# Attention scores of four heads in two pairs, with the first pair's maxima ahead of the Mamba scan

## The chip, the cores and the metric

One NeuronCore of one Trainium2 chip runs the whole kernel as one program. The metric is device time in microseconds (us), here the median of several executions; lower is better.

Five engines work side by side, each through its own list of instructions in the order written: PE (matrix multiplies and transposes, in the trace split into the multiply PE and its weight load PEld), DVE (vector), ACT (scalar), POOL (GpSimd) and SP (it only issues DMAs here). They meet through semaphores: an instruction raises a counter when it has finished (`then_inc`), and another engine's list stops at `wait_ge` until the counter is high enough. What stands behind a wait in a list waits too.

## The reference

One decoder layer, float32, batch 4, sequence 256, hidden 256. Three blocks, each followed by a residual add and a layer norm:

```python
x = layernorm(x + attention(x))               # 16 heads of 16, causal softmax, Wo at the end
x = layernorm(x + mamba(ctx, gate=silu(x)))   # conv + selective scan, 256 channels, 16 states, length 256
x = layernorm(x + moe(x))                     # softmax router, top 2 of 8 experts, 512 inner
```

In the attention, `scores = Q K^T / 4` under a causal mask, `attn = softmax(scores)`, `out = attn V`. In the scan, for each of 256 channels and 16 states, `state_t = exp(delta_t * A) * state_(t-1) + delta_t * u_t * B_t`, and `y_t = sum over states of state_t * C_t`.

## The kernel before

The attention and the scan don't depend on each other, so the kernel interleaves them. The main part is a loop over 4 batches `b` and, inside, 8 steps `m`; `g = 8*b + m` numbers the steps, and each step scans two of the 16 states. In steps m = 0 to 3 of a batch the four groups of heads, `G = 4*b + m`, are also scored: a group has four heads `r`, each with its own PSUM bank of `psS`. There is no scheduler. The order on each engine is written out by hand in one loop per engine, and what follows is what the change touches.

PE, step m: `scores(G)` writes the causal mask into the four banks with four matmuls (L1357, one per head, each waiting for that head's exponentials of the group before, since these read the bank), then adds QK^T for queries 0 to 127 (L1361) and for queries 128 to 255 (L1365), four heads each, every head on its own 32 rows of the array, and raises `score_ps` once. Then `broadcast_b(g+1, n)` (L1337) spreads B of the next step's two states over the partitions into `psD[n]`; it waits for the scan (g, n), which reads the same bank. Then `turn_back(G-2)` (L1397) and `transpose_probs(G-1, j)` for j = 0, 1, 2 (L1379), each of which waits until ACT has copied the previous one out of `psT`, and `weigh_values(G-1)` (L1390).

DVE, step m: `multiply_b(g)` (L972, two halves) multiplies `psD` by delta*u; `scan(g)` (L981, two instructions) runs the recurrence from `psD` into `states`; `maxima(G)` takes the negated row maxima of all four heads in two reduces (L987 for 128 keys, L988 for 256 keys) and raises `max_rdy` once. Behind them come, by step, `add_gated` (L1036), `finish_delta`, `normalise` (L994, L995) and `gating` (L1026). Only in the very first step do the maxima stand ahead of the scan.

ACT, step m: `decay(g+2)` (L689) makes the scan's decay factors; then, in turn, `take_probT(G-1, 0)` (L727, the copy out of `psT`), `exponentials(G, 0)` (L718 and L719), `take_probT(G-1, 1)`, `exponentials(G, 1)`, `take_probT(G-1, 2)`, `exponentials(G, 2)` and `(G, 3)`, and `take_o(G-1)` (L731). Each `exponentials(G, r)` waits for `max_rdy`, that is for the maxima of all four heads.

POOL, step m: `multiply_c(g)` (L504 and on) takes the states that the scan left, and now and then the small layer norm operations (`inverse_deviation`, L491 to L494), which ACT's `normalise_rows` (L740) waits for.

After the loop come the router, the sorting of tokens to experts and 23 tiles of expert work, which the change doesn't touch.

Of the kernel before, what the change touches and what calls it, by code (L numbers as in the profile page):

```python
# [10 lines left out]
ALU = mybir.AluOpType  # L11
ACT = mybir.ActivationFunctionType
AX_X = mybir.AxisListType.X

P = 128
# [35 lines left out]
def decoder_layer(  # L51
# [28 lines left out]
    B, S, HID = x.shape  # L80
# [13 lines left out]
    SCORE = P + S  # L94
# [6 lines left out]
    GROUPS = 4  # L101
    GH = HEADS // GROUPS
# [10 lines left out]
    with ExitStack() as stack:  # L113
# [14 lines left out]
        ident_b = sb("ident_b", [P, P], BF16)  # L128
        mask_qk = sb("mask_qk", [P, P], BF16)
# [42 lines left out]
        q_m = sb("q_m", [P, 2, FC, S])  # L172
        k_sb = sb("k_sb", [P, FC, S])
        v_sb = sb("v_sb", [P, QC, HEADS, BC])
        negmax = sb("negmax", [P, 2, QC, GH])
# [417 lines left out]
        def _(act):  # L593
# [117 lines left out]

            def exponentials(G, r):
                H = GH * G + r
                act.wait_ge(max_rdy, G + 1)
                if G >= 2:

                    act.wait_ge(probT_ps, 3 * (G - 1))
                act.activation(probs_q[:, H % PR, 0:P], psS[:, r, 0:P], ACT.Exp, bias=negmax[:, G % 2, 0, r:r + 1])  # L718
                act.activation(probs_q[:, H % PR, P:], psS[:, r, P:SCORE], ACT.Exp,  # L719
                               bias=negmax[:, G % 2, 1, r:r + 1]).then_inc(prob_rdy, 1)  # L720
# [38 lines left out]
            for b in range(B):  # L759
                f = b - 1  # L760
                for m in range(NP):
                    g = NP * b + m
# [104 lines left out]
        def _(dve):  # L867
# [106 lines left out]
            def scan(g):  # L974
                if g >= ST:

                    dve.wait_ge(y_sum, g - ST + 1)
                for n in range(2):
                    dve.wait_ge(b_used, 2 * g + n + 1)
                    dve.wait_ge(dA_rdy, 4 * g + 2 * n + 2)  # L980
                    dve.tensor_tensor_scan(  # L981
                        states[:, g % ST, n].rearrange("p h s -> p (h s)"), dA[:, g % DA, n].rearrange("p h s -> p (h s)"),
                        psD[:, n, :], 0.0, ALU.mult, ALU.add).then_inc(scanned, 1)

            def maxima(G):
                dve.wait_ge(score_ps, G + 1)
                dve.tensor_reduce(negmax[:, G % 2, 0], psS[:, :, 0:P], AX_X, ALU.max, negate=True)  # L987
                dve.tensor_reduce(negmax[:, G % 2, 1], psS[:, :, P:SCORE], AX_X, ALU.max, negate=True).then_inc(max_rdy, 1)  # L988

            def normalise(G):  # L990
                t, a = divmod(G % GROUPS, 2)
# [53 lines left out]
            for b in range(B):  # L1045
                f = b - 1
                for m in range(NP):
                    g = NP * b + m
                    multiply_b(g)
                    if g == 0:  # L1050
                        maxima(0)
                    scan(g)
                    if m == 3 and f >= 0:
                        add_gated(f)
                    if 0 < m < GROUPS or g > 0 and m == 0:
                        maxima(GROUPS * b + m)
                    if 0 < g < B:
                        finish_delta(g)
                    if 2 <= m <= 5:
                        normalise(GROUPS * b + m - 2)  # L1060
                    if m == 1 and f >= 0:
                        gating(f)
                    elif m == 6:
                        if f >= 0:
                            take_logits(f)
                    elif m == 7:
                        residual(b)
# [172 lines left out]
        def _(pe):  # L1240
# [99 lines left out]
            def scores(G):  # L1340
                b, g = divmod(G, GROUPS)
                t, a = divmod(g, 2)
                if g == 0:
                    pe.wait_ge(q_rdy, 2 * (b + 1))
                    pe.wait_ge(k_rdy, b + 1)
                    pe.wait_ge(v_rdy, b + 1)
                    if b > 0:
                        pe.wait_ge(res_rdy, b)
                if G == 0:
                    pe.wait_ge(mask_rdy, 1)  # L1350
                    pe.wait_ge(abs_rdy, TH)
                    pe.wait_ge(relu_rdy, TH * HALVES)
                for r in range(GH):
                    if g > 0:

                        pe.wait_ge(prob_rdy, GH * (G - 1) + r + 1)
                    pe.matmul(psS[:, r, 0:2 * S].rearrange("p (j n) -> p j n", n=S)[:, :, 0:P], ident_b[:],  # L1357
                              mask_qk[:].rearrange("p (o n) -> p o n", o=1).broadcast_to([P, 2, P]), start=True, stop=True)
                for r in range(GH):
                    rows = slice(32 * r, 32 * r + 32)  # L1360
                    pe.matmul(psS[:, r, 0:P], q_m[rows, a, t, 0:P], k_sb[rows, t, 0:P], start=False, stop=True,  # L1361
                              skip_group_check=True)
                for r in range(GH):
                    rows = slice(32 * r, 32 * r + 32)
                    ins = pe.matmul(psS[:, r, P:SCORE], q_m[rows, a, t, P:S], k_sb[rows, t, :], start=False, stop=True,  # L1365
                                    skip_group_check=True)
                ins.then_inc(score_ps, 1)

            def take_turn(use):

# [321 lines left out]
```

## Time and profile before

| what | value |
|---|---|
| median of 3 runs (lowest, highest) | 428.7 us (428.37, 428.83) |
| the profiled execution, its own time | 431.48 us |
| its span, first to last instruction | 429.7 us |
| busy: PE, DVE, POOL, ACT | 340.4, 252.1, 248.5, 209.9 us |
| mean granted TensorE clock | 0.878 of full speed |
| loop over batches and steps, by DVE's first multiply to its last scan | about 34 to 237 us |
| expert work | about 270 to 406 us |

Busy time is time in instructions, without waits. In the loop (half of the span) no engine is always busy, so what counts there is which engine waits for which, and when. In the timeline rows of the section below the columns are: start and length in us, engine, line, operation, what it writes and reads, how many instructions the row merges, and in brackets how long the engine had stood idle before it and who released it. In rows by stretch they are: the stretch, its length, busy us (and count) of PE, PEld, DVE, ACT and POOL, the granted clock as a share of full speed, DMA share and GB/s. In rows of waits: engine, tile and line that waited, for whom, total us, times, longest. SPq means DMAs that SP issues.

### The profile page before, as it was taken

To read this page: it belongs to the slowest core of one execution; us is meant where nothing else is said; L and a number is where in the kernel's file an instruction comes from. 1 tells how busy PE (TensorE), PEld (TensorE's weight loads), DVE (VectorE), ACT (ScalarE), POOL (GpSimd) and SP (SyncE) were. 2 spreads that over 40 slices of the span, in tenths; PEclk is the share of its full clock that TensorE was granted. 3 is DMA by queue.
4 is the path that set the end of the run, shared out by engine and by line. 5 is a ranking of instruction groups with operands and counts; after the bars stand their busy time and mean duration, and the time that the engine had idled before them with its cause. 6 is when DMAs were issued, how large, how long until landed. Compare 5 with 4: busy or idle time off the path is not lost.

```text
span 429.7 us, 5678 instructions
## 1 busy us (share of the span) xinstructions
PE 340.4 (79%) x1780; PEld 205.5 (48%) x1780; DVE 252.1 (59%) x439; ACT 209.9 (49%) x488; POOL 248.5 (58%) x232
## 2 busy tenths in 40 slices
PE   8794868856778677875869586899999999999651
PEld 4352435623446244653435242466666666666441
DVE  2989797974958879688977676112122222222134
ACT  4678786737877678767964100322222222212103
POOL 2075999999978996789888302233233333331214
PEclk9986596965989769896986888999999999999967
DMA  7050110162114510242106950111111111111162
GB/s 209 8 101 3 38 35 31 47 219 50 50 50 82 188 50 26 65 148 84 51 24 218 374 193 0 49 41 46 37 51 49 50 49 37 50 37 38 37 195 99
DMA packets 29455, 34.46 MB, mean 80 GB/s; under 512 B 4074, under 2 KB 23826, under 8 KB 29426
## 3 DMA queue, kind: packets, MB, share of 16 engines
q1 hardware_dynamic: 24770, 26.36, 20.3%
q0 software_dynamic: 2208, 6.03, 4.6%
q10 hardware_dynamic: 2448, 1.71, 1.4%
q8 instruction: 15, 0.25, 0.2%
q14 instruction: 14, 0.11, 0.1%
HBM read 28.92 MB, written 5.18 MB: 79 GB/s over the span
## 4 chain that ended last, share of the span: by engine, by line
PE 36%; DVE 6%; DMA 2%; ACT 2%; POOL 2%; issue 2%; DVEq 0%; POOLq 0%; ACTq 0%
PE psS L1600 18%; PE psD L1619 5%; PE psO L1619 4%; PE psD L1610 2%; PE psS L1450 2%; PE psT L1595 1%; DMA c_rows<-z_out 1%; DVE experts L981 1%; POOL rstd L493 1%; DVE u_sb L1131 1%; PE psT L1379 1%; DMA delta<-x_rows,row_in 1%; DMA z_out<-delta,row_out 1%; PE psT L1444 0%; POOL rstd L492 0%
## 5 line engine op out<-in xcount | busy, mean ns | idle before, releaser
L1600 PE MATMUL psS<-experts,delta 128*128 x184 | 86.5, 593 | 0.5 <-ACT delta L818 0.5
L504 POOL TENSOR_TENSOR experts<-experts,c_rows 128x1024 f32<-128x1024 f32 x31 | 73.0, 2355 | 17.8 <-DVE experts L981 17.4
L981 DVE TENSOR_TENSOR_SCAN experts<-experts,psD 128x512 f32<-128x512 f32 x64 | 74.4, 1204 | 0.0
L572 POOL DMA_INDIRECT z_out<-delta,row_out x23 | 22.8, 991 | 88.4 <-ACT delta L832 88.4
L1379 PE MATMUL psT<-ident,probs_at 128*128 128x128 f32 x192 | 39.2, 340 | 23.4 <-ACT probT L727 23.4
L1205 DVE COPY u_sb<-psD 128x512 f32<-128x512 f32 x23 | 15.9, 692 | 68.7 <-PE psD L1610 68.7
L689 ACT ACTIVATE experts<-delta,A_sb 128x255 f32<-128x255 f32 x128 | 54.7, 517 | 0.5 <-DVE du L929 0.5
L972 DVE TENSOR_TENSOR psD<-du,psD 128x512 f32<-128x512 f32 x64 | 41.6, 688 | 13.2 <-PE psD L1337 12.9
L1600 PEld LDWEIGHTS psS<-experts,delta 128*128 128x128 f32 x184 | 33.1, 190 | 24.3 <-issue 23.3
L1379 PEld LDWEIGHTS psT<-ident,probs_at 128*128 128x128 f32 x192 | 27.4, 172 | 35.1 <-ACT probT L727 33.4
L507 POOL TENSOR_TENSOR experts<-experts 128x512 f32<-128x512 f32 x31 | 40.7, 1312 | 2.4
L515 POOL TENSOR_TENSOR y_sb<-y_sb,experts 128x512 f32<-128x512 f32 x31 | 39.8, 1282 | 2.4
L727 ACT COPY probT<-psT 128x512 f32<-128x512 f32 x48 | 28.2, 587 | 22.3 <-PE psT L1379 21.2
L1213 DVE TENSOR_TENSOR du<-du,psS 128x512 f32<-128x512 f32 x23 | 15.8, 688 | 37.2 <-PE psS L1600 37.2
L1337 PE MATMUL psD<-bc_parts,rows_b 96*128 96x512 bf16 x64 | 25.5, 454 | 9.2 <-DVE experts L981 9.0
L719 ACT ACTIVATE probs_at<-psS,negmax 128x256 f32<-128x256 f32 x64 | 31.0, 484 | 0.0
L718 ACT ACTIVATE probs_at<-psS,negmax 128x128 f32<-128x128 f32 x64 | 24.1, 377 | 12.3 <-DVE negmax L988 11.8
L566 POOL DMA_INDIRECT delta<-x_rows,row_in x23 | 22.6, 982 | 10.1 <-issue 6.8
L825 ACT ACTIVATE du<-psS 128x512 f32<-128x512 f32 x23 | 13.7, 598 | 29.5 <-PE psS L1600 29.5
L1357 PE MATMUL psS<-mask_qk,ident_b 128*128 128x256 bf16 x64 | 15.1, 332 | 12.4 <-ACT probs_at L719 9.0
L1619 PE MATMUL psD<-experts,u_sb 128*128 x96 | 22.8, 380 | 0.9 <-DVE u_sb L1205 0.9
L832 ACT COPY delta<-psD 128x256 f32<-128x256 f32 x12 | 4.5, 372 | 36.7 <-PE psD L1619 36.7
(236 smaller groups left out, 591.6 us busy)
## 6 DMA issues: line engine op xcount, KB each, us to landing
c_rows<-c_dram SPq DMA_DIRECT2D x32, 256.0 KB, 3.4
experts<-in_L_ffn_w_gate_dram SPq DMA_DIRECT2D x8, 512.0 KB, 5.9
experts<-in_L_ffn_w_up_dram SPq DMA_DIRECT2D x8, 512.0 KB, 6.9
experts<-in_L_ffn_w_down_dram SPq DMA_DIRECT2D x8, 512.0 KB, 8.1
x_in<-in_x_dram SPq DMA_DIRECT2D x4, 256.0 KB, 5.3
x_rows<-x_sb SPq DMA_DIRECT2D x4, 256.0 KB, 2.5
probs_at<-z_out SPq DMA_DIRECT2D x4, 256.0 KB, 5.1
c_rows<-z_out ACTq DMA_DIRECT2D x4, 256.0 KB, 6.3
```

The costliest lines, as they stand in the source:

```text
L504: pool.tensor_tensor(states[:, g % ST], states[:, g % ST], c_rows[:, g % CR].rearrange("p n (o s) -> p n o s", o=1).broadcast_to([P, 2, HA ...
L507: pool.tensor_tensor(states[:, g % ST, 0], states[:, g % ST, 0], states[:, g % ST, 1], ALU.add).then_inc(pair_rdy, 1)
L515: pool.tensor_tensor(y_sb[:, b % 2], y_sb[:, b % 2], states[:, g % ST, 0], ALU.add).then_inc(y_sum, 1)
L689: act.activation(dA[:, g % DA, n, half, 1:], delta[:, b, half, 1:], ACT.Exp, scale=A_sb[:, half, 2 * m + n:2 * m + n + 1]).then_inc(dA_rdy, 1)
L719: act.activation(probs_q[:, H % PR, P:], psS[:, r, P:SCORE], ACT.Exp, bias=negmax[:, G % 2, 1, r:r + 1]).then_inc(prob_rdy, 1)
L727: act.copy(probT[:, j], psT[:].rearrange("p (h n) -> p h n", h=GH)).then_inc(psT_taken, 1)
L972: dve.tensor_tensor(halves(psD[:, n, :]), du[:, b], halves(psD[:, n, :]), ALU.mult).then_inc(b_used, 1)
L981: dve.tensor_tensor_scan(states[:, g % ST, n].rearrange("p h s -> p (h s)"), dA[:, g % DA, n].rearrange("p h s -> p (h s)"), psD[:, n, :], ...
L1337: pe.matmul(halves(psD[:, n, :]), pick(2 * m + n), wide(bc_parts[:, b * S:(b + 1) * S]).broadcast_to([3 * BC, HALVES, S]), start=True, sto ...
L1379: ins = pe.transpose(psT[:, r * P:(r + 1) * P], probs_q[:, (GH * G + r) % PR, j * P:(j + 1) * P], ident[:])
L1600: ins = pe.matmul(psS[:, bank, :], xgT[:, s % 2, k, :], gate_up_of(bass.ds(e, 1), i)[:, k, :], start=(k == 0), stop=(k == FC - 1))
L1619: ins = pe.matmul(y_bank(s), hgT[:, s % 2, c, :], down_of(bass.ds(e, 1))[:, c, :], start=(c == 0), stop=(c == IC - 1))
```

## The change

Each group of four heads is now handled in two pairs, heads 0 and 1, then heads 2 and 3. PE does mask, QK^T of the first query half and of the second for a pair and raises `score_ps`, then does the same for the other pair; the wait on the previous group's exponentials is one per pair. DVE takes a pair's maxima in two reduces of half the size, and raises `max_rdy` once per pair. The first pair's maxima stand between `multiply_b(g)` and `scan(g)`, the second pair's directly behind `scan(g)` (before, all four stood behind the scan, and in m = 3 behind `add_gated` too). ACT's exponentials of heads 0 and 1 wait for the first pair's maxima, those of heads 2 and 3 for the second's.

```diff
             def exponentials(G, r):
                 H = GH * G + r
-                act.wait_ge(max_rdy, G + 1)
+                act.wait_ge(max_rdy, 2 * G + r // 2 + 1)
...
-            def maxima(G):
-                dve.wait_ge(score_ps, G + 1)
-                dve.tensor_reduce(negmax[:, G % 2, 0], psS[:, :, 0:P], AX_X, ALU.max, negate=True)
-                dve.tensor_reduce(negmax[:, G % 2, 1], psS[:, :, P:SCORE], AX_X, ALU.max, negate=True).then_inc(max_rdy, 1)
+            def maxima(G, pair):
+                heads = slice(2 * pair, 2 * pair + 2)
+                dve.wait_ge(score_ps, 2 * G + pair + 1)
+                dve.tensor_reduce(negmax[:, G % 2, 0, heads], psS[:, heads, 0:P], AX_X, ALU.max, negate=True)
+                dve.tensor_reduce(negmax[:, G % 2, 1, heads], psS[:, heads, P:SCORE], AX_X, ALU.max,
+                                  negate=True).then_inc(max_rdy, 1)
...
                     multiply_b(g)
-                    if g == 0:
-                        maxima(0)
+                    if m < GROUPS:
+                        maxima(GROUPS * b + m, 0)
                     scan(g)
+                    if m < GROUPS:
+                        maxima(GROUPS * b + m, 1)
                     if m == 3 and f >= 0:
                         add_gated(f)
-                    if 0 < m < GROUPS or g > 0 and m == 0:
-                        maxima(GROUPS * b + m)
...
-                for r in range(GH):
+                for pair in ((0, 1), (2, 3)):
                     if g > 0:
 
-                        pe.wait_ge(prob_rdy, GH * (G - 1) + r + 1)
-                    pe.matmul(psS[:, r, 0:2 * S].rearrange("p (j n) -> p j n", n=S)[:, :, 0:P], ident_b[:],
-                              mask_qk[:].rearrange("p (o n) -> p o n", o=1).broadcast_to([P, 2, P]), start=True, stop=True)
-                for r in range(GH):
-                    rows = slice(32 * r, 32 * r + 32)
-                    pe.matmul(psS[:, r, 0:P], q_m[rows, a, t, 0:P], k_sb[rows, t, 0:P], start=False, stop=True,
-                              skip_group_check=True)
-                for r in range(GH):
-                    rows = slice(32 * r, 32 * r + 32)
-                    ins = pe.matmul(psS[:, r, P:SCORE], q_m[rows, a, t, P:S], k_sb[rows, t, :], start=False, stop=True,
-                                    skip_group_check=True)
-                ins.then_inc(score_ps, 1)
+                        pe.wait_ge(prob_rdy, GH * (G - 1) + pair[1] + 1)
+                    for r in pair:
+                        pe.matmul(psS[:, r, 0:2 * S].rearrange("p (j n) -> p j n", n=S)[:, :, 0:P], ident_b[:],
+                                  mask_qk[:].rearrange("p (o n) -> p o n", o=1).broadcast_to([P, 2, P]), start=True, stop=True)
+                    for r in pair:
+                        rows = slice(32 * r, 32 * r + 32)
+                        pe.matmul(psS[:, r, 0:P], q_m[rows, a, t, 0:P], k_sb[rows, t, 0:P], start=False, stop=True,
+                                  skip_group_check=True)
+                    for r in pair:
+                        rows = slice(32 * r, 32 * r + 32)
+                        ins = pe.matmul(psS[:, r, P:SCORE], q_m[rows, a, t, P:S], k_sb[rows, t, :], start=False, stop=True,
+                                        skip_group_check=True)
+                    ins.then_inc(score_ps, 1)
```

What this makes of PE's order in a step with scores is shown for m = 2. Before, from the scores of the group to the values (`rows_b` and `bc_parts` are the operands of the broadcast of B):

```order
L1357 MATMUL psS<-mask_qk,ident_b 128x2x128 x4
L1361 MATMUL psS<-k_sb,q_m 128x128 x4
L1365 MATMUL psS<-k_sb,q_m 128x256 x4
L1337 MATMUL psD<-bc_parts,rows_b 128x512 x2
L1397 MATMUL psO<-ident,oT_sb 128x128 x2
L1379 MATMUL psT<-ident,probs_at 128x128 x12
```

The same place now (lines 1360, 1364, 1368 are those of mask and QK^T in the changed kernel, L1339 is the broadcast, L1400 and L1382 are `turn_back` and the transposes):

```order
L1360 MATMUL psS<-mask_qk,ident_b 128x2x128 x2
L1364 MATMUL psS<-k_sb,q_m 128x128 x2
L1368 MATMUL psS<-k_sb,q_m 128x256 x2
L1360 MATMUL psS<-mask_qk,ident_b 128x2x128 x2
L1364 MATMUL psS<-k_sb,q_m 128x128 x2
L1368 MATMUL psS<-k_sb,q_m 128x256 x2
L1339 MATMUL psD<-bc_parts,rows_b 128x512 x2
L1400 MATMUL psO<-ident,oT_sb 128x128 x2
L1382 MATMUL psT<-ident,probs_at 128x128 x12
```

The three rows of scores became six; the broadcasts, `turn_back` and the transposes stand behind them as before.

DVE in the same step m = 2 of a later batch, before (L981, the scan, is listed as SCALAR_TENSOR_TENSOR):

```order
L972 TENSOR_TENSOR psD<-du,psD 128x512 x2
L981 SCALAR_TENSOR_TENSOR experts<-experts,psD 128x512 x2
L987 TENSOR_REDUCE negmax<-psS 128x4
L988 TENSOR_REDUCE negmax<-psS 128x4
L994 RECIPROCAL recip<-psO 128x8
L995 TENSOR_TENSOR o_sb<-psO,recip 128x2x4x16
```

And now:

```order
L972 TENSOR_TENSOR psD<-du,psD 128x512 x2
L988 TENSOR_REDUCE negmax<-psS 128x2
L989 TENSOR_REDUCE negmax<-psS 128x2
L981 SCALAR_TENSOR_TENSOR experts<-experts,psD 128x512 x2
L988 TENSOR_REDUCE negmax<-psS 128x2
L989 TENSOR_REDUCE negmax<-psS 128x2
L996 RECIPROCAL recip<-psO 128x8
L997 TENSOR_TENSOR o_sb<-psO,recip 128x2x4x16
```

Two reduces, with a wait for the first pair's scores in front of them, moved from behind the scan to ahead of it.

## Rows read from the trace of the kernel before

**Rows 1.** Who waited for whom, whole span, three of the rows

```profile
PEld psD L1337 <- DVE experts L981: 14.3, 14, 5.4
DVE negmax L987 <- PE psS L1365: 14.0, 7, 4.6
...
ACT probs_at L718 <- DVE negmax L988: 11.8, 7, 3.2
```

**Rows 2.** Busy time by stretch: the whole of batch 2

```profile
138.70:190.00 51.30, 38.52 (x272) 24.02 (x272) 41.62 (x62) 38.26 (x96) 43.24 (x34) 0.83 0.26 81
```

**Rows 3.** Timeline of batch 2, step m = 2 and the start of m = 3

```profile
153.34 2.32 DVE L981 TENSOR_TENSOR_SCAN experts<-experts,psD 128x512 f32<-128x512 f32 x2
...
155.39 1.03 PE L1357 MATMUL psS<-mask_qk,ident_b 128*128 128x256 bf16 x4
...
158.02 0.69 DVE L987 TENSOR_REDUCE negmax<-psS 128x4 f32<-128x512 f32 x1 [2.36 <-PE psS L1365]
...
158.63 1.22 DVE L988 TENSOR_REDUCE negmax<-psS 128x4 f32<-128x1024 f32 x1
159.18 0.59 ACT L727 COPY probT<-psT 128x512 f32<-128x512 f32 x1 [1.42 <-PE psT L1379]
...
163.33 0.70 PE L1357 MATMUL psS<-mask_qk,ident_b 128*128 128x256 bf16 x4
163.55 0.40 ACT L731 COPY oT_sb<-psO 128x256 f32<-128x256 f32 x1
...
164.82 0.61 PE L1337 MATMUL psD<-bc_parts,rows_b 96*128 96x512 bf16 x2
...
166.12 0.59 ACT L727 COPY probT<-psT 128x512 f32<-128x512 f32 x1 [0.58 <-PE psT L1379]
...
170.81 0.40 ACT L731 COPY oT_sb<-psO 128x256 f32<-128x256 f32 x1
```

**Rows 4.** Timeline of batch 2, step m = 0

```profile
139.44 0.60 PE L1357 MATMUL psS<-mask_qk,ident_b 128*128 128x256 bf16 x4 [0.94 <-ACT v_sb L709]
139.89 2.33 DVE L981 TENSOR_TENSOR_SCAN experts<-experts,psD 128x512 f32<-128x512 f32 x2
139.97 0.50 PE L1361 MATMUL psS<-k_sb,q_m 32*128 32x128 f32 x8
...
140.30 0.61 PE L1365 MATMUL psS<-k_sb,q_m 32*128 32x256 f32 x8
...
141.16 0.39 PE L1337 MATMUL psD<-bc_parts,rows_b 96*128 96x512 bf16 x1 [0.25 <-DVE experts L981]
...
142.28 0.39 PE L1337 MATMUL psD<-bc_parts,rows_b 96*128 96x512 bf16 x1 [0.72 <-DVE experts L981]
...
143.97 0.37 ACT L718 ACTIVATE probs_at<-psS,negmax 128x128 f32<-128x128 f32 x1 [3.17 <-DVE negmax L988]
```

**Rows 5.** Timeline of batch 2, step m = 1

```profile
146.95 0.81 PE L1361 MATMUL psS<-k_sb,q_m 32*128 32x128 f32 x8
147.54 1.08 PE L1365 MATMUL psS<-k_sb,q_m 32*128 32x256 f32 x8
...
150.47 0.59 ACT L727 COPY probT<-psT 128x512 f32<-128x512 f32 x1 [0.67 <-PE psT L1379]
...
155.77 0.40 ACT L731 COPY oT_sb<-psO 128x256 f32<-128x256 f32 x1
```

**Rows 6.** Groups by line: QK^T of the first query half, all 128 passes

```profile
L1361 PE MATMUL psS<-k_sb,q_m 32*128 32x128 f32 x128 | 10.2, 398 | 0.0
```

**Rows 7.** Timeline of batch 1, m = 0 to 1: the layer norm wait

```profile
94.37 1.06 PE L1379 MATMUL psT<-ident,probs_at 128*128 128x128 f32 x4
...
95.85 1.09 ACT L740 ACTIVATE x<-x,shift,rstd 128x256 f32<-128x256 f32 x2 [4.29 <-POOL shift L494]
...
99.10 0.56 ACT L727 COPY probT<-psT 128x512 f32<-128x512 f32 x1
```

**Rows 8.** Busy time by stretch: a stretch of batch 2 at lower clock

```profile
144.10:157.70 13.60, 10.90 (x70) 5.65 (x70) 10.24 (x11) 11.76 (x31) 13.22 (x9) 0.50 0.18 49
```

## The prediction

> **What bounds the kernel now.** I read the page first: the loop over batches and steps fills half of the span, and in it no engine is busy all the time, so shares of busy time decide nothing. In batch 2 (51.3 us) POOL is busy 43.2, DVE 41.6, PE 38.5 and ACT 38.3 us [rows 2]. Next I read the waits of the whole span [rows 1]. DVE stood idle for 14.0 us, 7 times, for a group's scores, and ACT for 11.8 us, 7 times, for maxima. These two the change aims at. The third row matters as much: PE's weight load for the broadcast of B waited 14.3 us, 14 times, for a scan. Then I read the timeline of one batch, to see what closes the loop from one group of heads to the next.
>
> I call E the moment when ACT has issued a group's last exponential; it is the start of the copy L731. In batch 2 E falls at 155.77, 163.55 and 170.81 us [rows 3]. Between two of them runs this circle: PE makes the next group's scores, then the two broadcasts, then the first transposes of the finished group's probabilities; ACT copies these out (L727), and then exponentials and copies alternate up to the next E. From that first copy to E it takes 163.55 - 159.18 = 4.37 us at full clock, and 155.77 - 150.47 = 5.30 us at the lower level [rows 3, 5]. The periods are 7.78 us (m = 2) and 7.26 us (m = 3). The scan is not in this circle: that of m = 2 ran from 153.34 to 155.66, and the scores ended only just before DVE took them up at 158.02, so both broadcasts found their banks free and ran together [rows 3]. In other words, the scan lies in the time in which DVE would otherwise wait for the scores.
>
> **The change, part by part.**
>
> *DVE's extra reduces.* The first reduce (512 columns) is followed by the second after 0.61 us, and the second, with 512 columns more, lasts 0.53 us longer [rows 3]. So a column costs about 1.04 ns and an instruction some 0.08 us beside it. A pair's two reduces take 0.34 + 0.61 = 0.95 us. Two pairs add under 0.2 us a group, 3 us in 16 groups, and mostly where DVE waits anyway. I book them only where they stand in the circle.
>
> *PE's scores in pairs.* For four heads the masks start at 139.44 and QK^T at 139.97; the last of it ends at 140.30 + 0.61 = 140.91, so QK^T lasts 0.94 us at full clock, and 147.54 + 1.08 - 146.95 = 1.67 us at half [rows 4, 5]. Is a pair shorter? The 128 passes of L1361 last 398 ns each, 50.9 us together, but PE was busy with them for 10.2 us only [rows 6]: the heads run side by side, each on its own rows of the array. So a pair takes as long as four heads; what it saves is two masks, 0.1 us each (0.2 at half). A pair is ready 0.32 + 0.94 = 1.26 us after its first mask at full clock, and about 0.5 + 1.67 = 2.2 us at half. If instead the passes shared one stream, a pair would be ready about 0.45 us sooner at full clock and 0.8 at half. I take the first, since an overlap of five passes is in the row, and keep the second for the lower end: with two steps per batch at half and one at full it is 4 x (0.8 + 0.8 + 0.45) = 8 us less.
>
> The Trainium skill says the same of the array ("TensorEngine Tiling (Array Packing)", Key Properties: tiles of 32 rows work independently and in parallel), and it has a rule that speaks against this change: a switch of tiling mode drains the array. Each pair goes from the mask's full rows to 32 rows and back, so there are two switches more per group. By the rule and the skill's independence, splitting gains nothing in the array and PE pays the short-row part twice; by the view of one shared stream the sum would be the 8 us lower. The row on overlap agrees with the first; what a drain costs no row shows by itself.
>
> PE's second pair costs about 1.2 us more of PE per group, but it lies beside DVE's maxima and scan (3.3 us), so I book it at nothing. If that cover were gone, it would be 16 x 1.2 = 19 us.
>
> *The moved maxima: the new wait.* This is the term that decides. DVE now waits, behind `multiply_b(g)`, for the first pair's scores; queued behind this wait are the scan of the step, the second maxima, `normalise` and the next multiply. And PE's two broadcasts stand in its list behind both pairs of scores and wait for that scan; behind them stand the transposes that ACT's copy waits for. So the scan enters the circle. From a scan's start to the second broadcast it is 142.28 - 139.89 = 2.39 us [rows 4]. From the second broadcast to ACT's copy it is 166.12 - 164.82 less 0.22 between the broadcasts (0.61 for two, 0.39 for one) = 1.08 us [rows 3, 4]; at half clock about 1.4, since there the whole way from the end of the scores to the copy is 150.47 - 148.62 = 1.85 us with one more broadcast in it [rows 5].
>
> The new period of m = 3, at full clock, counted from E: the first mask stands at -0.22 (163.33 against 163.55); first pair ready 1.26; DVE takes it up 0.08 later (an allowance of mine for the semaphore, too small to decide anything); maxima 0.95; scan to second broadcast 2.39; to the copy 1.08; to the next E 4.37. That is 9.91 us against 7.26: **+2.65**. In m = 2 the first mask stands at -0.38 (155.39) and the pair falls in the stretch at half clock [rows 8], 2.2: 10.69 against 7.78: **+2.9**.
>
> In m = 0 the scan moves from 139.89 to 139.44 + 1.26 + 0.08 + 0.95 = 141.73. ACT starts the first two exponentials there, 2.2 us sooner than at 143.97 [rows 4], but heads 2 and 3 wait for the maxima behind the scan, so E is hardly earlier. The second broadcast is at 144.12, and only then can PE begin the scores of m = 1 (about 144.35, at half clock): pair ready 146.55, scan at 147.58, second broadcast 149.97, copy 151.4 against 150.47: **+0.9** for m = 1 [rows 5].
>
> Steps 4 to 7 have no scores and keep their form; they start later by the whole sum, with DVE's and PE's lists late alike, so nothing is won back.
>
> A batch: 0.9 + 2.9 + 2.65 = 6.45 us. Four batches, which have the same order: 25.8 us. One cover exists: in batch 1 ACT waited 4.29 us for POOL's layer norm numbers, and its first copy ran at 99.10, though the transposes had ended at 94.37 + 1.06 = 95.43 [rows 7]. So the first 3.7 us of lateness from batch 0 are hidden. Left: **22.1 us**. The profiled execution took 431.48 us, 2.8 more than the median of the runs; it becomes 453.6, the median 450.8. I say 451.
>
> **The rivals.**
>
> *Faster, the change does what it seems to be for.* Where ACT waited for maxima in m = 0 (3.17 us in batch 2), its exponentials start 2.2 us sooner. If E followed, three later batches would gain 6.7 us: 422 us. For it speak the 11.8 and 14.0 us of waits [rows 1]. It holds only from the point where the second pair's maxima and the next broadcasts don't come later than before, which means that the first pair's scores must be there when `multiply_b` ends. In m = 2 that multiply ended before 153.34, and the first mask ran at 155.39 [rows 3].
>
> *No change.* POOL sets the pace and hides all. It was 84% busy in batch 2, and it would have to be late at each batch's end. Then 429 us.
>
> *Slower by less.* Only m = 3 pays in full, because in m = 1 and 2 DVE idled before its maxima anyway: 4 x 2.65 - 3.7 = 7 us, 436. Against it: that idle time began after the scan, not before it.
>
> *Slower by more, through the clock.* PE now has gaps of some 2 us in each of these steps, during the scan. In batch 2 the granted clock was 0.50, the 1.2 GHz level, from 144.10 to 157.70 us, behind a time in which PE did little but wait [rows 8]. If m = 2 and 3 ran at that level too, m = 3 would cost 0.94 (pair, 2.2 - 1.26), 0.93 (copy to E) and 0.3 more, 2.2 us, and m = 2 another 1.2: 4 x 3.4 = 13.7 us, 465 us. The Trainium skill ("TensorE: Matmul & The Clock Gate", HAM oscillation) has this as a rule: bursts of matmuls with waits between them fall back to the lower clock. The stretch at half clock agrees; that the new gaps suffice no row shows.
>
> **How the numbers follow.** Forecast (443 to 460 us) 0.60; through the clock (460 to 470) 0.20; slower by less (432 to 443) 0.12; faster 0.05; no change 0.03. The range 438 to 466 leaves out the two small cases, and the ends of the third and of the clock's, some 2 in 10; it holds the 8 us for a quicker pair. Under 0.2% (0.9 us) a difference can't be told here: faster 0.05, same 0.03, slower 0.92.
>
> **What the profile of the changed kernel would show.** Right: DVE's wait before the first pair's maxima (L988 of the new file) grows from 14.0 us to some 30 and more, in nearly all 16 steps with scores; PE's waits for the scan before the broadcasts (L1339) grow likewise; E to E is 9.4 to 10.7 us in m = 2 and 3; the expert part keeps its length. ACT's wait for maxima shrinks, that for the transposes grows. Wrong: the first pair's QK^T in half the time; scans that still start right behind the multiply; or a granted clock over the loop well off the 0.83 of [rows 2].

## The result, and the profile after

| | before | changed |
|---|---|---|
| median of 4 runs (lowest, highest) | 428.76 us (428.37, 430.04) | 475.6 us (474.33, 477.79) |
| the profiled execution, its own time | 431.48 us | 475.19 us |
| its span | 429.7 us | 473.4 us |
| mean granted clock | 0.878 | 0.792 |

The changed kernel takes 1.109 times as long (95%: 1.104 to 1.114). It is 46.8 us slower where 22 were forecast, and 475.6 lies above the range of 438 to 466.

Where the time went, I read first by E, the start of L731. From the E of m = 4 in one batch to that in the next it was, before, 52.8, 51.3 and 50.3 us; now 62.5, 64.2 and 64.6. The whole difference is made in the loop, where the last E falls 273.19 - 227.31 = 45.9 us later (the forecast for it was 22.1). From the last of these E's to the end of the span it is 429.7 - 227.3 = 202.4 us before and 473.4 - 273.2 = 200.2 now.

Rows by stretch, with columns as in [rows 2] and [rows 8]: the whole loop, the stretch of batch 2 at the lower level, and the whole of batch 2.

```profile
34.00:283.00 249.00, 198.88 (x1042) 115.33 (x1039) 172.21 (x268) 147.56 (x368) 178.50 (x141) 0.65 0.21 64
...
163.50:207.90 44.40, 36.87 (x184) 20.41 (x184) 27.62 (x45) 24.54 (x62) 26.86 (x20) 0.50 0.11 30
...
157.49:221.68 64.19, 51.84 (x272) 30.94 (x272) 42.85 (x71) 38.45 (x96) 43.24 (x34) 0.65 0.22 66
```

Batch 2 grew from 51.3 to 64.2 us, and its clock fell from 0.83 to 0.65. PE's 272 matmuls took 38.52 us before and take 51.84 now, while POOL's 34 take 43.24 in both. The stretch at 0.50, the 1.2 GHz level, was 13.6 us long; it is 44.4 us now and covers m = 1 to 3 and most of m = 4. PE is busy for 36.87 of these 44.4 us. It is not idle; it works, waits for a scan, and works again.

The waits of the changed kernel (engine, tile and line, for whom, total us, times, longest), to be set beside [rows 1]:

```profile
ACT probT L727 <- PE psT L1382: 74.7, 43, 6.8
...
POOL experts L504 <- DVE experts L981: 61.8, 16, 8.3
DVE negmax L988 <- PE psS L1368: 49.3, 14, 7.2
...
PEld psD L1339 <- DVE experts L981: 36.4, 36, 2.6
...
ACT probs_at L718 <- DVE negmax L989: 10.2, 7, 1.8
```

ACT's wait for maxima, which the change aims at, shrank by 1.6 us. DVE's wait for scores rose from 14.0 to 49.3, PE's for the scan before the broadcasts from 14.3 to 36.4. POOL now waits 61.8 us for scans. ACT waits 74.7 us for the transposes, which before was:

```profile
ACT probT L727 <- PE psT L1379: 21.2, 24, 1.5
```

The circle of m = 3 in batch 2 of the changed kernel, from one E (187.43) to the next (201.56):

```profile
187.43 0.40 ACT L731 COPY oT_sb<-psO 128x256 f32<-128x256 f32 x1
...
187.96 0.63 PE L1360 MATMUL psS<-mask_qk,ident_b 128*128 128x256 bf16 x2
...
190.23 0.42 DVE L988 TENSOR_REDUCE negmax<-psS 128x2 f32<-128x256 f32 x1 [7.20 <-PE psS L1368]
...
191.16 2.32 DVE L981 TENSOR_TENSOR_SCAN experts<-experts,psD 128x512 f32<-128x512 f32 x2
...
193.54 0.61 PE L1339 MATMUL psD<-bc_parts,rows_b 96*128 96x512 bf16 x1 [0.50 <-DVE experts L981]
...
194.31 0.68 DVE L1038 TENSOR_TENSOR x_sb<-psT,x 128x512 f32<-128x512 f32 x1
...
195.15 1.08 PE L1382 MATMUL psT<-ident,probs_at 128*128 128x128 f32 x4 [0.57 <-DVE x_sb L1038]
...
196.27 0.59 ACT L727 COPY probT<-psT 128x512 f32<-128x512 f32 x1 [6.85 <-PE psT L1382]
...
201.56 0.40 ACT L731 COPY oT_sb<-psO 128x256 f32<-128x256 f32 x1
```

The releaser in each bracket is the link before it. DVE stands 7.20 us before the first pair's maxima. The scan follows them, the broadcasts follow the scan, and the transposes come behind. ACT stands 6.85 us. The links are those of the prediction but for one: the transposes wait last for `add_gated` (L1038), which reads the bank `psT` that they write, and stands on DVE behind the held scan and the second maxima.

### The profile page after: what moved, and what is told of

Same layout as the page of the kernel before. It is cut to its first block, busy times and chain, and to the rows that moved or that the text cites. A ratio compares the mean times of both kernels' runs of the same rounds, so it can differ in the third digit from the quotient of the medians.

```text
span 473.4 us, 5710 instructions
## 1 busy us (share of the span) xinstructions
PE 389.2 (82%) x1780; PEld 229.8 (49%) x1780; DVE 256.1 (54%) x471; ACT 210.3 (44%) x488; POOL 248.8 (53%) x232
## 4 chain that ended last, share of the span: by engine, by line
PE 59%; DVE 17%; ACT 11%; issue 6%; POOL 4%; DMA 2%; DVEq 0%; POOLq 0%; ACTq 0%
PE psS L1603 17%; PE psT L1382 10%; DVE experts L981 8%; PE psD L1622 4%; PE psO L1622 4%; ACT probT L727 4%; DVE negmax L989 3%; PE psD L1339 2%; ACT experts L689 2%; PE psD L1613 2%; PE psO L1393 2%; PE psS L1368 2%; PE psS L1364 1%; PE psS L1321 1%; ACT probs_at L718 1%
## 5 line engine op out<-in xcount | busy, mean ns | idle before, releaser
L504 POOL TENSOR_TENSOR experts<-experts,c_rows 128x1024 f32<-128x1024 f32 x31 | 73.4, 2367 | 61.9 <-DVE experts L981 61.8
L981 DVE TENSOR_TENSOR_SCAN experts<-experts,psD 128x512 f32<-128x512 f32 x64 | 74.3, 1203 | 0.0
L1382 PE MATMUL psT<-ident,probs_at 128*128 128x128 f32 x192 | 52.4, 428 | 19.4 <-ACT probT L727 17.7
L727 ACT COPY probT<-psT 128x512 f32<-128x512 f32 x48 | 28.1, 586 | 74.9 <-PE psT L1382 74.7
L1382 PEld LDWEIGHTS psT<-ident,probs_at 128*128 128x128 f32 x192 | 36.7, 220 | 34.2 <-ACT probT L727 30.7
L1339 PE MATMUL psD<-bc_parts,rows_b 96*128 96x512 bf16 x64 | 30.7, 504 | 18.8 <-DVE experts L981 17.5
L988 DVE TENSOR_REDUCE negmax<-psS 128x2 f32<-128x256 f32 x32 | 13.2, 412 | 49.4 <-PE psS L1368 49.3
L1368 PE MATMUL psS<-k_sb,q_m 32*128 32x256 f32 x128 | 28.6, 536 | 0.0
L1339 PEld LDWEIGHTS psD<-bc_parts,rows_b 96*128 96x128 bf16 x64 | 6.9, 108 | 37.5 <-DVE experts L981 36.4
```

What stands on the lines that cost most here:

```text
L504: pool.tensor_tensor(states[:, g % ST], states[:, g % ST], c_rows[:, g % CR].rearrange("p n (o s) -> p n o s", o=1).broadcast_to([P, 2, HA ...
L727: act.copy(probT[:, j], psT[:].rearrange("p (h n) -> p h n", h=GH)).then_inc(psT_taken, 1)
L981: dve.tensor_tensor_scan(states[:, g % ST, n].rearrange("p h s -> p (h s)"), dA[:, g % DA, n].rearrange("p h s -> p (h s)"), psD[:, n, :], ...
L1339: pe.matmul(halves(psD[:, n, :]), pick(2 * m + n), wide(bc_parts[:, b * S:(b + 1) * S]).broadcast_to([3 * BC, HALVES, S]), start=True, sto ...
L1382: ins = pe.transpose(psT[:, r * P:(r + 1) * P], probs_q[:, (GH * G + r) % PR, j * P:(j + 1) * P], ident[:])
```

## The experiments

All ratios are to the kernel before, in the same session (its medians there were 428.1 to 430.0 us), with the 95% interval in brackets. "The held scan" means the scan that waits behind the first pair's scores.

**e1_scan_first.** Only DVE's order is put back; pairs and their signals stay. (Lines run one or two ahead of those of the changed kernel where an edit moves them.)

```diff
                     multiply_b(g)
-                    if m < GROUPS:
-                        maxima(GROUPS * b + m, 0)
                     scan(g)
-                    if m < GROUPS:
-                        maxima(GROUPS * b + m, 1)
                     if m == 3 and f >= 0:
                         add_gated(f)
+                    if m < GROUPS:
+                        maxima(GROUPS * b + m, 0)
+                        maxima(GROUPS * b + m, 1)
```

> The changed kernel with DVE's old order: the scan stands directly behind the multiply again, and both pairs' maxima behind it (behind add_gated in m = 3); PE's scores stay in two pairs. Theory A (the scan, held behind the wait for the first pair's scores, entered the circle from one group to the next, and the clock fell with it): most of the 47 us comes back. What stays is the second pair's longer score part, since four heads cost 1.47 us of PE at full clock and two pairs 2.4: 0.9 us per step at full clock, 1.7 at half, less the 3.7 us of cover: 436 to 446 us. Rival B (the split of the scores itself costs the time, through PE's work and mode switches): it stays within 10 us of 475.6. Rival C (only where the scan stands counts, the pairs cost nothing): 427 to 431.

Measured: 448.15 us, 1.041 (1.038, 1.044). That is 2 us above what I expected. The place of two reduces cost 27.5 us of the 46.8. Some 18 stay without it: pairs cost something by themselves. They stand mainly in m = 2, which takes 11.51 us from E to E in batch 2 (7.78 in the kernel before). The weight loads' wait for the scan before the broadcasts is 6.5 us (36.4 in the changed kernel). In m = 2 of batch 2, in its timeline:

```profile
161.71 0.80 PE L1363 MATMUL psS<-k_sb,q_m 32*128 32x128 f32 x4
...
162.29 1.06 PE L1367 MATMUL psS<-k_sb,q_m 32*128 32x256 f32 x4
...
163.29 0.61 PE L1359 MATMUL psS<-mask_qk,ident_b 128*128 128x256 bf16 x2
...
163.82 0.80 PE L1363 MATMUL psS<-k_sb,q_m 32*128 32x128 f32 x4
...
164.41 1.06 PE L1367 MATMUL psS<-k_sb,q_m 32*128 32x256 f32 x4
```

At this clock four heads took 0.81 and 1.08 us [rows 5]; a pair takes 0.80 and 1.06. The second pair is late by 163.82 - 161.71 = 2.11 us.

**e2_four_ahead.** The other half: the kernel before, PE unsplit, with all four heads' maxima moved ahead of the scan.

```diff
-                    if g == 0:
-                        maxima(0)
+                    if m < GROUPS:
+                        maxima(GROUPS * b + m)
                     scan(g)
...
-                    if 0 < m < GROUPS or g > 0 and m == 0:
-                        maxima(GROUPS * b + m)
```

> The kernel before, with PE's scores of four heads at once as they were, and the maxima of all four heads moved ahead of the scan in every step with scores. Theory A: the circle holds the whole score part, 1.74 us of maxima and 2.39 us from scan to second broadcast; against the changed kernel each step is longer by about 1.1 us (the two reduces are 0.8 us longer, the scores 0.3), so 480 to 490 us. Rival B (the split of PE's scores is the cost): clearly below 475, near 440 to 450, since nothing is split here.

Measured: 491.79 us, 1.143 (1.141, 1.145). That is 2 us above the upper end of what I expected. The place alone costs 62 us, with nothing split; the changed kernel, whose scan waits for two heads and not for four, is 16 us faster.

**e3_broadcast_late.** The changed kernel, with PE's broadcasts of m = 1 to 3 behind the first and the second transposes, so that ACT's first copy no longer stands behind the scan.

```diff
-                    if m < GROUPS:
+                    if m == 0:
...
-                        if m == 4:
-                            broadcast_b(g + 1, 0)
+                        broadcast_b(g + 1, 0)
```

(and the same for the second broadcast.)

> The changed kernel, but in steps m = 1 to 3 PE's two broadcasts of B stand behind the first and the second set of transposes of probabilities, as they already do in m = 4. DVE keeps the new order, so the scan still waits for the first pair's scores. Theory A: the way from a group's last exponential to ACT's first copy no longer holds the scan; the period of m = 2 falls from 12.4 to about 9, of m = 3 from 14.1 to 11 (add_gated, behind the scan, still holds the transposes of m = 3), and the clock stays higher: 440 to 455 us. Rival D (DVE's lateness as such is the bound: scan, maxima and multiply must follow each other, whoever waits for the broadcasts): 465 us or more.

Measured: 448.06 us, 1.042 (1.038, 1.046). By this other edit 27.5 us come back too, so in the changed kernel the placement is dear mainly by the way through PE's broadcasts. That both edits give the same sum is chance, for what is left stands elsewhere. In batch 2, E to E of m = 2 is 7.77 us, as before the change (7.78), but that of m = 3 is 12.40 (7.26). Over the four batches m = 3 is 20 us longer than before. In three of them the transposes wait there for `add_gated`, which is still behind the held scan (the first batch has none):

```profile
PE psT L1382 <- DVE x_sb L1038: 10.2, 3, 3.4
...
175.36 1.09 PE L1382 MATMUL psT<-ident,probs_at 128*128 128x128 f32 x4 [3.42 <-DVE x_sb L1038]
```

(a row of waits, whole span, and one of the timeline of m = 3, batch 2).

**e4_filled.** The changed kernel with bf16 matmuls of 256 columns in PE's gaps around the broadcasts, and in m = 1 behind the transposes. They are extra work; nothing reads what they write.

```diff
+            def fill(n, cols):
+                for _ in range(n):
+                    pe.matmul(psO[:, cols].rearrange("p (k n) -> p k n", n=P), ident_b[:],
+                              mask_qk[:].rearrange("p (o n) -> p o n", o=1).broadcast_to([P, S // P, P]),
+                              start=True, stop=True)
...
+                        if m >= 2:
+                            pe.wait_ge(o_rdy, G - 1)
+                        fill(6, slice(S, 2 * S))
                         broadcast_b(g + 1, 0)
+                        fill(3, slice(S, 2 * S))
                         broadcast_b(g + 1, 1)
```

> The changed kernel plus matmuls whose result nobody reads (bf16, 256 columns, into psO) in PE's gaps: 6 ahead of the first broadcast and 3 between the two in m = 0 to 3, and 3 behind each of the first two sets of transposes in m = 1. Nothing else moves. Theory A with the clock as half of the loss: if these keep the granted clock of the loop at the upper level, each step with scores gets 2 to 3.5 us shorter, up to 24 us in all, 450 to 460 us. If the clock falls all the same, the 9 dummies cost up to 1.5 us of PE per step at half clock, partly beside the scan: 475 to 490. If the clock rises and the time doesn't fall, the clock was no cause.

Measured: 450.4 us, 1.043 (1.037, 1.050), so 25 us less with more work. Its loop:

```profile
34.00:260.00 226.00, 180.92 (x1212) 110.99 (x1209) 173.18 (x269) 147.92 (x368) 178.37 (x140) 0.87 0.23 71
```

The clock is 0.87 against 0.65. In batch 2, E to E is 9.35 us for m = 2 and 11.02 for m = 3 (12.39 and 14.13 in the changed kernel; forecast 10.69 and 9.91 us), and both now run at full clock:

```profile
165.79:175.14 9.35, 7.19 (x63) 4.05 (x61) 5.78 (x10) 6.12 (x17) 5.32 (x4) 1.00 0.13 30
175.14:186.16 11.02, 7.22 (x61) 3.85 (x59) 9.59 (x17) 6.14 (x17) 6.08 (x7) 1.00 0.07 24
```

From the second broadcast to the copy it is 170.78 - 169.69 = 1.09 us in m = 2, as forecast, and 181.79 - 179.53 = 2.26 in m = 3, where the transposes wait for `add_gated`.

**e5_gated_first.** The changed kernel, `add_gated` between the scan and the second maxima.

> The changed kernel with add_gated, in m = 3, again directly behind the scan and ahead of the second pair's maxima. In the changed kernel PE's transposes of m = 3 waited 0.57 us for add_gated to read psT, and PE stood free for about 0.8 us before them, in three batches. Theory A (this is the term that the prediction missed): 2 to 3 us less than the changed kernel, 472 to 474. If the second maxima, now later, hold the exponentials of heads 2 and 3 instead: no gain, 475 to 477.

Measured: 473.99 us, 1.104 (1.102, 1.107): 1.6 us less than the changed kernel, and the two intervals overlap. This reaches `add_gated` only past the maxima, not past the held scan.

**e6_before_filled.** The kernel before with such fills in m = 0, 1 and 4.

> The kernel before plus matmuls whose result nobody reads (bf16, 256 columns), only where PE waits: in m = 0 four between the two broadcasts and twelve behind them, in m = 1 three behind each of the first two sets of transposes, in m = 4 six at the start. Theory A (the granted clock in the loop is worth microseconds wherever the circle runs over PE): the stretches at half clock, 78 us of the loop before, shrink, and the time falls to 418 to 427 us. Rival: DVE and POOL hold the loop and PE's clock is worth nothing here: 428 to 431; or the fills themselves delay PE: over 431.

Measured: 425.51 us, 0.990 (0.987, 0.993). Such fills give the kernel before some 4 us too, a sixth of what they give the changed one; its loop (34 to 237 us) shows a clock of 0.92 with them and 0.81 without.

**e7_masks_first.** As e1_scan_first, but PE writes the four masks first, each with its own wait, then QK^T of the first pair and of the second.

```diff
-                for pair in ((0, 1), (2, 3)):
+                for r in range(GH):
                     if g > 0:
-                        pe.wait_ge(prob_rdy, GH * (G - 1) + pair[1] + 1)
-                    for r in pair:
-                        pe.matmul(psS[:, r, 0:2 * S].rearrange("p (j n) -> p j n", n=S)[:, :, 0:P], ident_b[:],
+                        pe.wait_ge(prob_rdy, GH * (G - 1) + r + 1)
+                    pe.matmul(psS[:, r, 0:2 * S].rearrange("p (j n) -> p j n", n=S)[:, :, 0:P], ident_b[:],
...
+                for pair in ((0, 1), (2, 3)):
```

> As e1_scan_first (scan ahead of both pairs' maxima), but PE writes all four masks first, one per head and each behind its own head's exponentials as before the change, and then QK^T of pair 0 and of pair 1. So the pairs stay in QK^T, and the extra way back to the full array for two masks between the pairs is gone. If the price of the pairs is that way (masks and the end of one shape before the next): 430 to 438 us, against 448 for e1_scan_first. If it is that two heads take as long as four whatever stands between: 440 to 448.

Measured: 425.07 us, 0.991 (0.989, 0.994), 23 us under e1_scan_first and below both ranges that I had given. It is faster than the kernel before too, by 1%, a small difference but one that the interval keeps clear of 1. The timeline of m = 0, batch 2:

```profile
137.36 0.60 PE L1358 MATMUL psS<-mask_qk,ident_b 128*128 128x256 bf16 x4 [0.94 <-ACT v_sb L709]
...
137.88 0.52 PE L1363 MATMUL psS<-k_sb,q_m 32*128 32x128 f32 x8
...
138.21 0.63 PE L1367 MATMUL psS<-k_sb,q_m 32*128 32x256 f32 x8
...
141.07 0.37 ACT L718 ACTIVATE probs_at<-psS,negmax 128x128 f32<-128x128 f32 x1 [2.38 <-DVE negmax L989]
```

With nothing between them the two pairs take 0.52 and 0.63 us together, as four heads did at once [rows 4], and ACT's wait is 2.38 us where it was 3.17.

**e8_reduces_split.** As e7, with QK^T of all four at once and one signal for both pairs: PE does exactly what it did before.

> As e7_masks_first, but QK^T of four heads at once, as before the change, with score_ps raised by two at its end: PE's list is that of the kernel before, DVE's order too; only the reduces are four of half the size, and ACT waits by pairs. Theory A: two more reduces cost under 0.2 us a group and lie mostly in waits, ACT's first exponentials may start 0.8 us sooner in m = 3: 426 to 432 us. If many small reduces are dear: over 433.

Measured: 425.99 us, 0.993 (0.990, 0.995), at the lower end of the first range. It can't be told from e7. So the gain of both over the kernel before comes from the split of DVE's reduces and ACT's wait, not from the order in the array.

**e9_masks_first_ahead.** PE as in e7, DVE in the order of the change.

> PE as in e7_masks_first (four masks, then QK^T of pair 0 and of pair 1, which ran there in 0.94 us like four heads at once), DVE as in the changed kernel: the first pair's maxima ahead of the scan. So only the place of the maxima differs from e7_masks_first (425 us). Theory A: the period of m = 2 and 3 holds scores, 0.93 us of maxima, 2.39 us to the second broadcast and the way to the copy; that is the changed kernel's circle but for the wait on the masks of heads 2 and 3: 460 to 475 us. If the place were cheap once the pairs are cheap: under 445.

Measured: 484.13 us, 1.125 (1.120, 1.130), 9 above the upper end of what I expected, and 8.5 above the changed kernel. Here the first pair's scores stand behind the mask of head 3, which waits for the exponentials of head 3; the changed kernel asks only for heads 0 and 1. That shows mainly in m = 1, where those exponentials wait for the maxima behind the held scan: from E of m = 4 to E of m = 1 in batch 2 it is 184.88 - 151.88 = 33.00 us, and 175.04 - 144.46 = 30.58 in the changed kernel. With the maxima ahead of the scan, masks by pairs save 8.5 us; with the scan first, they cost 23.

**e10_masks_first_filled.** e7 with the fills of e6.

> e7_masks_first with the unread matmuls of e6_before_filled in m = 0, 1 and 4. The fills took 4.2 us off the kernel before, e7_masks_first 3.8 to 4.7. If the two gains add up: 419 to 423 us. If the fills only give what the shorter waits of e7_masks_first already gave through the clock (0.905 against 0.878): 424 to 426.

Measured: 422.67 us, 0.982 (0.978, 0.986), the fastest of all and in the range for gains that add up, though the 6.7 us are less than the sum of the two (4.7 and 4.3).

**e11_ahead_in_m0.** e7, but in m = 0 the first pair's maxima stand ahead of the scan: the one step in which PE's scores are nearly ready when the multiply ends (DVE waits 0.97 us for them).

> e7_masks_first, but in m = 0 of each batch the first pair's maxima stand ahead of the scan, the one step in which these scores are nearly ready when the multiply ends. ACT's first two exponentials start 1.4 us sooner, the scan 1.8 us later, and with it the second broadcast, which PE's scores of m = 1 stand behind. Theory A (heads 2 and 3 still wait for maxima behind the scan, and the next scores behind the broadcast): no gain, 425 to 430 us. If ACT's earlier start counts: 419 to 424.

Measured: 429.63 us, 1.000 (0.998, 1.002), 4.6 slower than e7. ACT starts its first exponentials after 1.22 us of wait instead of 2.38, and E gains nothing, because heads 2 and 3 and the next broadcasts come later: from the first multiply of batch 2 to E of m = 1 it is 152.45 - 135.46 = 16.99 us, and 152.87 - 136.62 = 16.25 in e7.

**e12_ahead_broadcast_late.** e9 with the late broadcasts of e3 and `add_gated` right behind the scan.

> e9_masks_first_ahead (484 us) with the two ways out of the circle: PE's broadcasts behind the first and second set of transposes in m = 1 to 3, as in e3_broadcast_late, and add_gated directly behind the scan, as in e5_gated_first. DVE's first maxima still stand ahead of the scan and the scan still waits for the scores. Theory A (the maxima's place costs only by way of PE's broadcasts and add_gated): 430 to 445 us. If the late scan as such holds the loop (scan, second maxima, multiply, POOL): 460 us or more.

Measured: 452.88 us, 1.057 (1.053, 1.060). It lies between the two expectations: of the 59 us between e9 and e7, 31 come back and 28 don't. Its waits say what holds these:

```profile
PE psT L1382 <- DVE x_sb L1038: 10.9, 3, 3.7
...
PE psO L1393 <- DVE o_sb L997: 8.2, 5, 4.1
```

In e7 the first is absent and the second 1.8 us. The timeline of e12's m = 3, batch 2:

```profile
175.99 2.32 DVE L981 TENSOR_TENSOR_SCAN experts<-experts,psD 128x512 f32<-128x512 f32 x2
178.23 0.67 DVE L1038 TENSOR_TENSOR x_sb<-psT,x 128x512 f32<-128x512 f32 x1
...
179.04 1.09 PE L1382 MATMUL psT<-ident,probs_at 128*128 128x128 f32 x4 [3.64 <-DVE x_sb L1038]
...
180.17 0.59 ACT L727 COPY probT<-psT 128x512 f32<-128x512 f32 x1 [5.88 <-PE psT L1382]
```

The broadcasts are out of the way, and the scan still holds the transposes, through `add_gated`. In this batch m = 2, which has no such reader, took 172.32 - 164.70 = 7.62 us from E to E (7.94 in e7); m = 3 took 185.46 - 172.32 = 13.14 (6.96 in e7). Over the four batches m = 3 holds 21.5 of the 28 us. In batch 0, which has no `add_gated`, it is `normalise` (L997) that comes late, behind the held scan and `finish_delta`, and PE's values wait for it in the same way, 3.13 us in m = 2 and 4.12 in m = 3.

## Why the prediction was wrong, point by point

**Right: direction and mechanism.** The scan entered the circle through the wait that now stands ahead of it. E to E grew in m = 2 and 3. e1, e3 and e2 each move the placement, or the way through which it acts, alone; each moves the time by 27 to 62 us. At full clock the circle is of the forecast length but for one term: in e4, m = 2 takes 9.35 us, where the prediction's pieces at full clock add up to 10.69 - 0.94 = 9.75, and m = 3 takes 11.02 for 9.91, the 1.1 more being `add_gated`.

**Right: the pieces that DVE times.** The maxima took 0.94 and 0.93 us (forecast 0.95), scan to second broadcast 2.38 (2.39). A pair's QK^T took as long as four heads', so the 8 us for a shared stream were rightly left out. The Trainium skill's rule that a switch of tiling mode drains the array ("TensorEngine Tiling (Array Packing)", Key Properties) agrees as far as e7 shows it: pairs overlap when no full-row mask stands between them, and don't when one does; what share of that is a drain no run here separates.

**The step that failed: the sum at full clock.** The prediction took m = 3 at full clock, m = 2 in part, and left the rest to a rival with a chance of 0.20. In the trace of batch 2 both ran at 0.50 from end to end (the forecast had it only in the scores of m = 2):

| piece of the circle | m = 2 forecast | measured | m = 3 forecast | measured |
|---|---|---|---|---|
| E to first mask | -0.38 | -0.38 | -0.22 | 0.53 |
| first mask to DVE's maxima | 2.28 | 2.24 | 1.34 | 2.27 |
| maxima | 0.95 | 0.94 | 0.95 | 0.93 |
| scan to second broadcast | 2.39 | 2.38 | 2.39 | 2.38 |
| second broadcast to copy L727 | 1.08 | 1.92 | 1.08 | 2.73 |
| copy L727 to E | 4.37 | 5.29 | 4.37 | 5.29 |
| sum | 10.69 | 12.39 | 9.91 | 14.13 |

For m = 2 the 1.70 us too few are all PE's pieces at half clock. For m = 3 they are 4.22; of these, 2.73 - 1.92 = 0.81 is `add_gated`, and 3.41 the clock, the 0.75 ahead of the mask included (the transposes of L1429 ran there at half clock). m = 4, booked as unchanged, took 7.08 us instead of 6.21: 0.87. Over all four batches, m = 2 and m = 3 exceed their forecasts by 3.5, 5.6, 5.9 and 5.9 us, 20.9 in all. Of these, 2.4 are `add_gated`; with 1.7 for m = 4 the clock has some 20 of the 23.8 us that the loop grew beyond the forecast (45.9 for 22.1). e4 shows that this is the clock: at full clock again, the pieces have their short lengths. That its 450.4 us lie next to the forecast of 451 is partly luck. Its fills also raise the clock where it was low before the change, which alone gave 4.3 us in e6, its m = 2 is shorter than forecast and its m = 3 longer.

**The rival "through the clock" was the case, and underpriced.** It named gaps in PE during the scan and the right steps, but gave 13.7 us (its terms add up to 13.6). It left out m = 4 and the way from E to the mask, and took 0.3 us for the piece from the broadcast to the copy, which grew by 0.84. A higher price alone would not have mended the forecast; its chance was too low. In the kernel before, the stretch of [rows 8] begins while PE stands idle: it had waited 0.25 and 0.72 us for the scan [rows 4], and now waits for exponentials:

```profile
144.75 0.40 PE L1357 MATMUL psS<-mask_qk,ident_b 128*128 128x256 bf16 x1 [2.09 <-ACT probs_at L719]
```

The change put waits for the scan into every step with scores.

**Missed: a second release behind the held scan.** The prediction listed the scan, the second maxima, `normalise` and the next multiply as queued on DVE behind the wait. It left out `add_gated`, and asked only of the scan who waits for it. `add_gated` releases `psT` for PE's transposes. In the changed kernel that adds only 0.81 us in m = 3 of three batches, since the broadcasts are nearly as late. With those out of the way it is a bound of its own: 3.42 us of PE's wait in e3, 3.64 in e12.

**Booked at nothing: PE's second pair.** In the changed order this held: PE waits for the scan anyway. The price "if that cover were gone", 19 us, lies next to the 18 us of e1, but by luck: it counts 1.2 us a group at full clock, and in e1 the second pair is 2.11 us late at half clock. Nor was the reason the one given, twice the work on 32 rows alone: e7 does both pairs too and pays nothing. It is the masks between the pairs, which keep them from overlapping, and their joint wait; the clock falls with it, 0.848 against 0.905 over the span. How those share the 23 us was not measured.

**m = 1 and the cover.** From the start of batch 2 to E of m = 1 it is 175.04 - 157.49 = 17.55 us, before 155.77 - 138.72 = 17.05: 0.5 where 0.9 was forecast. The 3.7 us of cover in batch 1 are in line with its smaller growth: E to E of m = 4 grew by 9.6 us there, by 12.9 and 14.3 in the next two.

**The rival that ended faster.** Its first half came true: in m = 0 ACT's wait for maxima fell from 3.17 to 1.00 us, 2.2 as worked out. E did not follow, and e11 shows that it doesn't follow even where only m = 0 is changed.

Of the signs named in advance, DVE's and PE's waits, the transposes, the pair's QK^T and the unchanged expert part came as written; E to E (12.4 and 14.1 against 9.4 to 10.7) and the clock (0.65 against 0.83) showed it wrong.

## What to carry to other kernels

Before a wait is put ahead of an operation in a hand-ordered list, follow each operation behind it on that engine, and ask of each whose buffer it releases; here PE waited for the scan, `add_gated` and `normalise` by turns, and with the first out of the way (e3) the next held it. Such a wait also broke PE's work into pieces at half clock here, so price such steps at both levels, and let the likelier one carry the sum. What was worth having was the finer signal, not the earlier place: split the reduces and the waits, leave the scan in front and matmuls of one shape together (e7, 429.77 - 425.07 = 4.7 us; with fills 429.41 - 422.67 = 6.7).

## What the runs showed of the hardware

Matmuls that nobody reads made the kernel faster: 25 us in the changed kernel, 4 in the one before. In batch 2 of the changed kernel PE was busy for 36.87 of 44.4 us (163.50 to 207.90) and the granted clock stayed at 0.50 throughout. Before it fell it was 1.00, and PE had stood idle for 1.07 and 0.72 us before the two broadcasts of m = 0.

Two heads on 32 rows each took as long as four (0.49 and 0.60 us against 0.50 and 0.61 [rows 4]):

```profile
158.53 0.49 PE L1364 MATMUL psS<-k_sb,q_m 32*128 32x128 f32 x4
...
158.85 0.60 PE L1368 MATMUL psS<-k_sb,q_m 32*128 32x256 f32 x4
```

(the changed kernel, m = 0 of batch 2), but two pairs in a row with no other shape between them took no longer than one.
